# Sixteen-entry decoder on one core: four entries in flight instead of three, with 18 weight matrices loaded for every entry

## The reference

```python
x = ln(x + L0_attn(x))          # linear attention per token over 16 heads, then a gelu MLP 256 -> 1024 -> 256
x = ln(x + L0_xattn(x, ctx))    # 16 heads, softmax within |i - j| <= 64
x = ln(x + L0_ffn(x))           # six nodes, each an 8-head softmax attention:
                                #   q, k, v = ew[c] * (nodes[..] @ We[..] + be[..])
                                #   nodes[c] = act_w[c] * mha(q, k, v, Wq[c], Wk[c], Wv[c], Wo[c]) + q
x = ln(x + L1_attn(x))          # q, v rms-normed per head; causal, out = q . cumsum(k v)
x = ln(x + L1_xattn(x, ctx, mask))   # 16 heads, q and k layer-normed per head, padded keys masked
x = ln(x + L1_ffn(x))           # real(ifft(fft(x) @ w)) + bias, folded to one 256 x 256 matrix
```

## Time and profile before

| what | value |
|---|---|
| median of 3 runs | 3996.06 us (3991.0 to 4010.05) |
| the profiled execution | 4006.72 us, its span 4005.0 us |
| mean granted TensorE clock in it | 0.931 |
| PE busy | 3573.8 us, 89% of the span, 35084 instructions |
| DVE, ACT, POOL busy | 1925.5, 1679.8, 947.2 us |
| DMA | 44.02 MB, 40 slices of which only the first is busy |

### The profile page before, as it was taken

One profiled execution on the slowest core, in us unless ns is written; L12 is line 12 of the kernel. 1 busy time (PEld: TensorE's weight loads), 2 busy tenths in 40 slices (PEclk: granted clock), 3 DMA queues, 4 the chain that ended last, 5 costly groups with the idle time before them and its releaser, 6 DMA issues.

```text
span 4005.0 us, 82977 instructions
## 1 busy us (share of the span) xinstructions
PE 3573.8 (89%) x35084; PEld 2593.2 (65%) x35084; DVE 1925.5 (48%) x3647; ACT 1679.8 (42%) x3338; POOL 947.2 (24%) x763
## 2 busy tenths in 40 slices
PE   6989889989888989899998999989898998988986
PEld 5766667666656766666675666756666675666654
DVE  4453453564455535555354645535455353642423
ACT  1234444444434444344444444444344443444432
POOL 6460040142203204040220503104040220500000
PEclk8989999999999999999998998999899998999987
DMA  6000000000000000000000000000000000000000
GB/s 212 20 1 4 1 9 4 10 4 9 4 1 9 4 10 4 9 4 1 10 4 9 4 1 9 4 10 4 9 4 1 10 4 9 4 1 4 4 6 3
DMA packets 40731, 44.02 MB, mean 11 GB/s; under 512 B 4656, under 2 KB 40240, under 8 KB 40240
## 3 DMA queue, kind: packets, MB, share of 16 engines
q1 hardware_dynamic: 40368, 38.72, 3.1%
HBM read 34.52 MB, written 4.19 MB: 10 GB/s over the span
## 4 chain that ended last, share of the span: by engine, by line
PE 72%; DVE 11%; issue 6%; ACT 6%; POOL 4%; DMA 0%; SPq 0%; DVEq 0%; ACTq 0%; POOLq 0%
PE banks L664 17%; PE banks L656 13%; PE banks L870 12%; PE banks L838 9%; DVE nmx L1168 7%; PE banks L811 5%; ACT work L1377 4%; PE banks L776 3%; PE banks L649 3%; POOL work L1526 2%; PE banks L842 2%; PE banks L671 2%; PE banks L943 2%; PE banks L822 1%; POOL work L1516 1%
## 5 line engine op out<-in xcount | busy, mean ns | idle before, releaser
L1168 DVE TENSOR_REDUCE nmx<-banks 128x4 f32<-128x1024 f32 (+1 forms) x640 | 717.2, 1165 | 338.6 <-PE banks L811 337.7
L664 PE MATMUL banks<-work,weights 128*128 128x256 f32 x3584 | 843.5, 385 | 9.1 <-ACT work L1276 7.4
L1377 ACT ACTIVATE work<-banks 128x1024 f32<-128x1024 f32 (+1 forms) x640 | 602.4, 980 | 531.2 <-PE banks L842 530.9
L664 PEld LDWEIGHTS banks<-work,weights 128*128 128x128 f32 x3584 | 667.9, 191 | 146.9 <-issue 49.1
L656 PE MATMUL banks<-weights,work 128*128 128x256 f32 x2688 | 658.4, 392 | 18.4 <-ACT work L1304 8.4
L656 PEld LDWEIGHTS banks<-weights,work 128*128 128x128 f32 x2688 | 505.1, 194 | 122.7 <-issue 42.5
L838 PE MATMUL banks<-work 32*128 32x256 f32 (+1 forms) x5120 | 466.2, 451 | 83.2 <-DVE nmx L1168 23.6
L1526 POOL TENSOR_TENSOR work<-work 128x512 f32<-128x512 f32 x256 | 385.1, 1522 | 174.2 <-DVE work L1134 164.4
L811 PE MATMUL banks<-work 32*128 32x256 f32 (+1 forms) x5120 | 356.0, 397 | 69.4 <-ACT work L1377 21.5
L1181 DVE TENSOR_TENSOR work<-banks,work 128x256 f32<-128x256 f32 x256 | 108.3, 423 | 643.7 <-ACT work L1387 643.4
L1553 POOL TENSOR_TENSOR work<-work,row 128x512 f32<-128x512 f32 x64 | 82.3, 1286 | 1320.5 <-PE banks L649 1320.5
(11 more groups left out here) (151 smaller groups left out, 3683.9 us busy)
## 6 DMA issues: line engine op xcount, KB each, us to landing
work<-in_w_setup SPq DMA_DIRECT2D x41, 256.0 KB, 5.9
work<-in_ctx SPq DMA_DIRECT2D x32, 256.0 KB, 3.0
work<-in_x SPq DMA_DIRECT2D x16, 256.0 KB, 2.9
out<-work SPq DMA_DIRECT2D x16, 256.0 KB, 2.2
weights<-in_w_all SPq DMA_DIRECT2D x1, 3072.0 KB, 16.5
weights<-in_w_all SPq DMA_DIRECT2D x2, 1024.0 KB, 10.4
weights<-in_w_all SPq DMA_DIRECT2D x1, 2048.0 KB, 16.9
row<-in_rows SPq DMA_DIRECT2D x1, 1664.0 KB, 7.5
```

Of the source, the lines that this page charges most:

```text
L664: ins = e.matmul(b[:, m * 256:m * 256 + 256], wslot(w)[:, k, m * P:m * P + P], xin[:, k, :], start=(k == 0 and (m == 0 or closed)) if star ...
L1168: e.tensor_reduce(nmax(s, n)[:, 2 * p:2 * p + 2, :], b, AX, ALU.max, negate=True).then_inc(*freed("max", n, p, i))
L1377: e.activation(dst, src, ACT.Exp).then_inc(*freed("exp", n, p, i))
```

## The change

Four entries are in flight (`NS = 4`), with a fourth set of slots. The first 18 weights of the list (those of the first attention, the MLP, the banded attention, and `r_q`, `r_v` of the causal one) are no longer kept. They are loaded for every entry, 256 KB at a time, into a ring of five buffers at the head of the tile `weights`, in the order in which TensorE uses them (289 loads with one for the setup). A load waits on SP until the fifth use before it is over; a product waits for its load (`arrived`). The other 16 loaded matrices and the 19 computed ones stay.

At most two long-held outputs are open (`LONG = 2`). Entries 0, 1 and 2 may start at once, entry 3 when the setup is over; the setup's operands lie in the fourth set. Setup steps count as entry 1.5 (2.5 on SP), and the planner's durations of `cb`, `nb`, `ob`, `n5` are longer. `eq` also waits for the exponentials of the quad before. The second quad of a pair waits for its own operands by name.

```diff
-NS = 3
+NS = 4
...
-            + ["x_q", "x_k", "x_v", "x_o"]
+            + ["x_q", "x_k", "x_v", "x_o", "r_q", "r_v"]
             + [f"{n}{c}" for c in range(NODES) for n in ("eq", "co")]
-            + ["r_q", "r_v", "y_q", "y_k", "y_v", "y_o"])
-W_GROUPS = {"a": (0, 4), "f": (4, 12), "x": (12, 16), "c": (16, 28), "y": (28, 34)}
+            + ["y_q", "y_k", "y_v", "y_o"])
+STREAMED = W_LOADED[:18]
+RING = 5
+W_GROUPS = {"c": (18, 30), "y": (30, 34)}
 W_COMPUTED = [f"{n}{c}" for c in range(NODES) for n in ("cq", "ck", "cv")] + ["fourier"]
-WSLOT = {n: i for i, n in enumerate(W_LOADED + W_COMPUTED)}
+WSLOT = {n: RING + i for i, n in enumerate(W_LOADED[18:] + W_COMPUTED)}
+USED_BY = {("a_qkv", 0): ("a_q",), ("a_qkv", 1): ("a_k",), ("a_qkv", 2): ("a_v",), ("a_o", 0): ("a_o",),
+           ("fc", 0): tuple(f"fc{j}" for j in range(4)), ("down", 0): tuple(f"proj{j}" for j in range(4)),
+           ("x_q", 0): ("x_q",), ("x_k", 0): ("x_k",), ("x_v", 0): ("x_v",), ("x_o", 0): ("x_o",), ("ob", 0): ("x_o",),
+           ("r_qv", 0): ("r_q",), ("r_qv", 1): ("r_v",)}
 
 W_SETUP = ["wr", "wi", "cos", "sin", "nsin"] + [f"{n}{c}" for c in range(NODES)
                                                 for n in ("eqT", "ekT", "evT", "wq", "wk", "wv")]
...
-SETUP0 = 2 * SLOTS
+SETUP0 = (NS - 1) * SLOTS
...
-BANKS, PAIRS, HALVES, LONG = 8, 4, 2, 3
+BANKS, PAIRS, HALVES, LONG = 8, 4, 2, 2
...
-        cb.append(folded("cb", c, 1.2, "DVE", 0.2, node[c]))
+        cb.append(folded("cb", c, 4.8, "DVE", 0.2, node[c]))
...
-    folded("nb", 0, 2.0, "DVE", 0.7, *scale, *cb)
-    folded("ob", 0, 1.75, "DVE", 0.8, w["x"], w["y"])
-    folded("n5", 0, 0.9, "DVE", 0.4, scale[5], cb[5])
+    folded("nb", 0, 10.4, "DVE", 0.7, *scale, *cb)
+    folded("ob", 0, 3.8, "DVE", 0.8, w["y"])
+    folded("n5", 0, 1.2, "DVE", 0.4, scale[5], cb[5])
...
-        eq = do("PE", "eq", c, 1.75, ("ACT", "exp", (5 + 2 * c, 1)), ("POOL", "scale", c), takes=("ctx",))
+        eq = do("PE", "eq", c, 1.75, ("ACT", "exp", (4 + 2 * c, 1)), ("ACT", "exp", (5 + 2 * c, 1)), ("POOL", "scale", c), takes=("ctx",))
...
-    events = [(0.0, 0, i, first) for i in range(2)] + [(0.0, 0, -1, n) for n in range(len(setup)) if not left[n]]
+    events = [(0.0, 0, i, first) for i in range(NS - 1)] + [(0.0, 0, -1, n) for n in range(len(setup)) if not left[n]]
...
-            for i, t, n in sorted(waiting[e], key=lambda w: (0.5 if w[0] < 0 else w[0], w[1], w[2])):
+            for i, t, n in sorted(waiting[e], key=lambda w: ((2.5 if e == "SP" else 1.5) if w[0] < 0 else w[0], w[1], w[2])):
...
+                started[e].append(now)
+                if e == "PE":
+                    names = USED_BY.get((op, a), ())
+                    used += [(w, i, now + us * (j + 1) / len(names)) for j, w in enumerate(names)]
...
-                    events += [(end, 0, j, first) for j in range(2, NS)]
+                    events.append((end, 0, NS - 1, first))
...
-    return plan
-
-
-PLAN = program_plan()
+    ring, loads = {}, []
+    for k, (w, i, t) in enumerate(used):
+        ring[w, i] = k % RING, used[k - RING][:2] if k >= RING else None
+        loads.append((used[k - RING][2] if k >= RING else 0.01, 1, (i, "stream", w, [])))
+    plan["SP"] = [step for _, _, step in sorted([(t, 0, step) for t, step in zip(started["SP"], plan["SP"])] + loads,
+                                                key=lambda v: v[:2])]
+    return plan, ring
+
+
+PLAN, STREAM = program_plan()
...
-        W = sb("weights", [P, len(WSLOT), NC, D])
+        W = sb("weights", [P, RING + len(WSLOT), NC, D])
...
+            def arrived(*names):
+
+                for w in names:
+                    e.wait_ge(*when("streamed", w, i))
+                    streamed_to[w] = STREAM[w, i][0]
...
-                    once("weights", "a")
-                    tokens(take("misc", "a_qkv", a, i), ("a_q", "a_k", "a_v")[a], slot(s, XT)).then_inc(
+                    w = ("a_q", "a_k", "a_v")[a]
+                    arrived(w)
+                    tokens(take("misc", "a_qkv", a, i), w, slot(s, XT)).then_inc(
...
-                    once("weights", "f")
                     for j in range(4):
                         if j % 2 == 0:
                             b = take("score", "gelu", j // 2, i)
+                        arrived(f"fc{j}")
                         features(b[:, j % 2, :], f"fc{j}", slot(s, XT)).then_inc(*tell(pe[s], "fc mm", j, i))
...
+                    arrived("proj0", "proj1", "proj2", "proj3")
...
+                elif op == "stream":
+                    r, earlier = STREAM[a, i]
+                    if earlier:
+                        e.wait_ge(*when(*used_by(*earlier)))
+                    row0 = W_LOADED.index(a) * D
+                    e.dma_start(W[:, r, :, :], w_all[row0:row0 + D, :].rearrange("(c p) n -> p c n", p=P)).then_inc(
+                        *tell(in_ring[r], "streamed", a, i))
...
-                    if i == 2:
+                    if i == NS - 1:
```

More of the change, by code:

```diff
@@ L166, in entry_steps @@
     z_t = through("z_t", 0, 0.44, "ACT", 0.72, z)
-    raw = [through("a_qkv", a, 1.75, "DVE", 0.66, z_t, ("PE", "ctx_t", 0), ("SP", "w", "a"), also=(ctx_t,))
+    raw = [through("a_qkv", a, 1.75, "DVE", 0.66, z_t, ("PE", "ctx_t", 0), also=(ctx_t,))
            for a in range(3)]
@@ L714, in tensor @@
                 elif op == "ob":
-                    once("weights", "x")
+                    arrived("x_o")
                     once("weights", "y")
@@ L914, in tensor @@
                         e.wait_ge(*when("r_t", i))
-                    once("weights", "y")
-                    tokens(take("misc", "r_qv", a, i), ("r_q", "r_v")[a], slot(s, XT)).then_inc(
+                    w = ("r_q", "r_v")[a]
+                    arrived(w)
+                    tokens(take("misc", "r_qv", a, i), w, slot(s, XT)).then_inc(
                         *tell(pe[s], "r_qv mm", a, i))
```

51 lines of the change are left out of this document (31 added, 20 removed).

## The result

The changed kernel takes 3825.05 us, median of 4 runs (3814.39 to 3826.79), against 3993.53 (3988.94 to 4010.05) for the kernel before: a ratio of 0.9565, 95% interval 0.9532 to 0.9598. It is 168 us faster where 73 were forecast. The direction held, and the time lies inside the range, but more than half of the gain was not foreseen: it goes past the 120 us that the prediction had as the sum of its good ends, and only the room left for a rival covers it.

The account below looks back on a forecast made before the run. PE bounds the kernel, busy 3573.8 of 4005.0 us with 431 idle. Idle -68, other engines +15, ring +5 and clock -25 sum to -73 us against 4006.7; forecast median 3923 us, range 3815 to 4005.

Parts of the forecast that it names:

- the sum of its good ends: Whole kernel: all terms at their best, -68 - 5 and 0.64 of that again for the clock, -120 us.
- The steady part, "+6": PE's steps 800 to 2199: gaps turn up elsewhere, so 6 us of idle time are added.
- The count: PE's steps laid end to end, charged for late needs: 408 us idle before, 340 after, trusted to about a tenth.
- The first rival: Steady part: a fourth entry also eases late DVE maxima, a quarter of 208 us goes; some 3840 us, chance 0.18.
- The start, -31 and -36: PE's steps 0 to 199 and 200 to 799: three entries starting instead of two cut idle time by 31 and 36 us.
- +15 for the other engines: First two parts: DVE, ACT and POOL are not always free, POOL's attention chains delaying PE; +15 us, between 0 and 34.
- The end, -7: PE's steps from 2200 on: idle time falls by 7 us; the last entry is alone for its last 65 steps.
- LONG = 2 "is in the count": PSUM banks: fewer single banks held, an upper pair free more often; no term beyond the late-needs estimate.
- The ring, +5: Streamed weights: some loads land late for PE, 1 to 15 us over the run, taken as +5.
- the slower rival: SP's queue: ring loads stuck behind late stores or context loads hold up PE; 120 us, 4043 us, chance 0.11.
- The clock, -25: PE's granted clock: 48 us less idle time gives back 0 to 31 us at 0.64 per idle us, taken as -25.
- the silent clock: PE's clock: rival that it gives nothing back, 3996 - 48 = 3948 us, chance 0.12.

Follow-up runs that it names:

- e1: Changed kernel with three entries in flight instead of four, all else as changed: 3941.69 us, 0.9835 of the kernel before.
- e2: Changed kernel with up to three long-held outputs instead of two: 3901.9 us, 0.9738 of the kernel before.
- e3: Changed kernel with the old start (two entries at once, the others after the setup, old setup priority): 3841.15 us, 0.9586 of the kernel before.
- e5: Kernel before with at most two long-held outputs instead of three, nothing else: 3945.03 us, 0.9856 of the kernel before.
- e6: Changed kernel with the planner's old setup durations and `eq` without its added need: 3848.51 us, 0.9617 of the kernel before.
- e8: Changed kernel with the planner's attention durations set to those of its trace: 3797.4 us, 0.9492 of the kernel before.
- e10: Kernel before with the planner's attention durations set to those measured in the trace: 3877.84 us, 0.9696 of the kernel before.
- e13: Changed kernel with measured planner durations and up to three long-held outputs: 3829.15 us, 0.9572 of the kernel before.
- e14: Changed kernel with two planner durations moved by 2% (`s` 0.95 to 0.97, `pv` 1.75 to 1.78): 3836.52 us, 0.959 of the kernel before.
- e12: Kernel before with measured planner durations and at most two long-held outputs: 3908.08 us, 0.9767 of the kernel before.
- e4: Changed kernel with only the first five ring loads, so its output is wrong: 3821.19 us, 0.9543 of the kernel before.
- e9: Kernel before, own order, with ten useless dense products at each of 308 places where PE tends to wait: 3938.8 us, 0.9855 of the kernel before.

## Why the prediction was right in sign and too small

Two terms of the sum failed: the idle time, -68 + 15 + 5 = -48 where -91 was measured, and the clock, -25 where PE's busy time fell by 90.

**The steady part, "+6".** This is the first step that failed. It was -39 us of idle time. The count met the order before within a tenth, and I took that for proof. For the order after, its total of 340 us is the trace's, but that is luck: part by part it is 39 us short at the start, where 20 of them were known to be lacking, 28 over in the steady part and 13 over at the end. Over the variants it gave 466 us (e1), 399 (e2), 371 (e3), 466 (e5), 396 (e6), 328 (e8), 429 (e10), 334 (e13) and 365 (e14), and the traces have 413, 394, 353, 428, 340, 327, 388, 339 and 372. Five of the nine it meets within 18 us; the others it puts 38 to 56 too high, which is more than most differences that it was to tell, and it had the wrong sign for e5 and e10. It takes DVE as free when needed, and at the two waits shown above DVE was full (5.31 of 5.50 us at one). The first rival, "The steady part gains too" at 3840, was what happened. The fourth entry is worth 117 us (e1). That this is DVE being late with something to fall back on was not isolated: the waits for a maximum fell by 75 us, which agrees, but in e5 they fall by 60 with no gain in idle time.

**The start, -31 and -36, and +15 for the other engines.** -11 and -33. The second is right. In the first 54 us stayed, where the count and the 20 us that it lacked make 35: 12.7 ahead of the first product, 9.7 for normalised inputs, some 10 for the setup's operands, the rest in small waits. The +15 fits in size, 18 us over the two parts. Its reason is not shown: POOL is busy for 234 of 399 us where it was 186 of 422, but no wait of PE for POOL is in the list of that part. The explanation by the start was wrong in the main: with the old one (e3) only 8 to 16 us are lost.

**The end, -7.** -9 us: right, and its clock stays at 0.86.

**LONG = 2 "is in the count".** Wrong. The limit gains 77 us here and some 60 with three entries (e5); with the measured durations it gains 32 with four entries (e13) and costs 30 with three (e12). So it has no fixed worth; as far as these runs show, it chooses another order.

**The ring, +5.** 0 to 4 us (e4), no wait of PE for it, 115 MB instead of the 121 that I had added up: the 18 matrices, 4.7 MB, no longer come at the start. Of the slower rival, a late queue, nothing is seen.

**The clock, -25.** This is the second step that failed, and the larger miss: PE's busy time fell by 90 us. The loss had been read right, 276 us, but was priced as 0.64 us for each idle us, as if all idle time were alike. The earlier trace rows spoke against that already: the second and the third part are both idle for 9% and lost 39 and 152 us, 0.45 and 0.73 for each idle us. From before to after the loss fell by 128 us for 91 idle us, 1.4 to one; in e5 by 66 for 3; between e6 and the change it differs by 30 at the same idle time, and in e14 it is 30 less at 31 more. So the loss is not set by how many us the waits sum to; that it is set by where they lie is what is left, and e9 agrees. Of the 128 lost us 110 fell on busy time, since a part of the low clock lies over idle time. The spread between runs of one and the same kernel goes with the clock too: seven runs of before on one chip go from 3984.2 us of span at a mean clock of 0.939 to 4011.9 at 0.929.

The Trainium skill ("TensorE: Matmul & The Clock Gate", Part 1: The HAM clock gate) puts the ramp at "<1% of a typical kernel span". It says this of the ramp at a kernel's start, and the prediction read it as a bound on all that the clock can cost. In that reading the silent clock at 3948 would have come out. Here 276 of 4005 us were lost, 7%, in 68 stretches over the whole span, and e9 gave 189 of them back with useless work. The sentence does not bear on a clock that falls again and again.

The sum as it should have been, for the span: -91 idle, -90 clock, 0 for the ring, 181 in all.

What stays open: which of the steady part's waits start a low stretch and which don't. The 2.8 us at 2416 are one that does. No rule was tested that would rank two orders ahead of a run, and the orders of e8 and e10 were found by better durations, not by a count.

## What to carry to other kernels

Where a bounding TensorE shows a mean clock under one, price a wait twice: its idle time, and the slower products that stand behind it; and do not expect the second to move with the first (here 128 us for 91, 66 for 3, and once the other way). An engine that is half idle over the span can be full for the few us that a wait depends on; read its time line there. A model of idle time that fits one order has shown nothing about its power to rank orders; fit it on two or three, or give it a range as wide as the clock's loss. Before another buffer, slot or limit is tried, give the planner the durations of the trace: here that alone gave 119 us to the old kernel and 28 to the new one, and with three entries it changed the sign of what the limit was worth.

## What had not been expected of the hardware

- More work made the kernel faster: 3160 useless products, 236 us of the bounding engine, for 68 us less of span (e9).
- The 1.2 GHz level outlasts the wait at whose end it begins: 14 us in which PE was busy for 12.55, with no gap over 0.42 us (the time line above).
- Two orders with 431 and 428 us of idle time lost 276 and 210 us to the clock (before and e5); one with 31 us more idle time than the change lost 30 us less (e14).
- 74 MB more through SP's queue, at 25 GB/s beside full work, moved nothing that could be measured (e4 against the change); a load of 256 KB landed in 2.7 us (the change).
